# The first two row tiles of a split matrix product run side by side for five column tiles of the second weights instead of four

## The reference

```python
def _L0_cond_ref(x, weight, bias, lora_a_weights, lora_b_weights, scaling_factors, adapter_id):
    base = einsum('bsi,oi->bso', x, weight) + bias
    low = einsum('bsi,bri->bsr', x, lora_a_weights[adapter_id])
    delta = einsum('bsr,bor->bso', low, lora_b_weights[adapter_id])
    return base + scaling_factors[adapter_id][:, None, None] * delta

def _L0_ffn_ref(x, W_base, b_base, W_router, lora_A, lora_B):
    # softmax over 8 router logits, the two largest renormalised to w
    h = einsum('td,erd->ter', xf, lora_A)
    lora_out = einsum('ter,eor,te->to', h, lora_B, w) * 2.0
    return x @ W_base.T + b_base + lora_out

x = x + _L0_ffn_ref(_L0_cond_ref(x, ...), ...)
x = x + _L1_ffn_ref(_L1_cond_ref(x, ...), ...)     # the same form, other weights
```

## Time and profile before

| | us |
|---|---|
| median of 3 runs | 687.23 |
| lowest and highest run | 686.88 and 687.95 |
| time of the profiled execution | 687.59 |
| span of the profiled execution, first to last instruction | 685.8 |
| TensorE matmul busy | 680.0 |
| VectorE busy | 421.5 |
| POOL busy | 261.3 |
| ScalarE busy | 233.5 |

### The profile page before, as it was taken

One profiled execution on the slowest core, in us unless ns is written; L12 is line 12 of the kernel. 1 busy time (PEld: TensorE's weight loads), 2 busy tenths in 40 slices (PEclk: granted clock), 3 DMA queues, 4 the chain that ended last, 5 costly groups with the idle time before them and its releaser, 6 DMA issues.

```text
span 685.8 us, 9221 instructions
## 1 busy us (share of the span) xinstructions
PE 680.0 (99%) x3309; PEld 600.7 (88%) x3309; DVE 421.5 (61%) x705; ACT 233.5 (34%) x429; POOL 261.3 (38%) x217
## 2 busy tenths in 40 slices
PE   8999999999999999999999999999999999999997
PEld 7999999888888888888899999998888888888886
DVE  5664668768855473862663753886698437738423
ACT  6444245644131034220514344266252302422200
POOL 2373023027593150395133432030647625105920
PEclk9999999999999999999999999999999999999999
DMA  8355756992868934547742755689836886535633
GB/s 298 109 159 180 261 198 209 390 380 108 263 186 321 343 117 130 157 141 258 281 170 72 231 169 183 246 275 375 332 122 216 291 333 195 175 117 171 192 113 122
DMA packets 74131, 147.24 MB, mean 215 GB/s; under 512 B 6948, under 2 KB 38308, under 8 KB 73958
## 3 DMA queue, kind: packets, MB, share of 16 engines
q1 hardware_dynamic: 70678, 138.20, 59.0%
q10 hardware_dynamic: 1872, 6.36, 3.0%
q0 software_dynamic: 1536, 2.10, 1.1%
HBM read 98.42 MB, written 47.33 MB: 213 GB/s over the span
## 4 chain that ended last, share of the span: by engine, by line
PE 97%; DMA 1%; SPq 1%; ACT 0%; DVE 0%; issue 0%
PE ps L599 45%; PE ps L481 15%; PE ps L482 15%; PE ps L483 15%; PE ps L558 4%; PE ps L615 2%; DMA e_raw<-in_ext 1%; PE ps L608 1%; SPq L281 0%; PE ps L498 0%; PE ps L581 0%; ACT e_hl L710 0%; SPq L258 0%; DVE w_hl L972 0%; DVE w L1177 0%; ACT w_hl L719 0%
## 5 line engine op out<-in xcount | busy, mean ns | idle before, releaser
L599 PE MATMUL ps<-x_hl,a_hl 128*128 128x512 f32 x1344 | 317.7, 394 | 0.0
L599 PEld LDWEIGHTS ps<-x_hl,a_hl 128*128 128x128 f32 x1344 | 251.1, 188 | 53.6 <-issue 0.3
L481 PE MATMUL ps<-e_hl,w_hl 128*128 128x384 f32 (+1 forms) x432 | 145.8, 338 | 0.6 <-DVE e_hl L972 0.5
L482 PE MATMUL ps<-e_hl,w_hl 128*128 128x384 f32 (+1 forms) x432 | 145.8, 338 | 0.0
L483 PE MATMUL ps<-e_hl,w_hl 128*128 128x384 f32 (+1 forms) x432 | 145.6, 337 | 0.0
L481 PEld LDWEIGHTS ps<-e_hl,w_hl 128*128 128x128 f32 x432 | 81.5, 189 | 1.8 <-issue 1.0
L482 PEld LDWEIGHTS ps<-e_hl,w_hl 128*128 128x128 f32 x432 | 81.4, 188 | 0.0
L483 PEld LDWEIGHTS ps<-e_hl,w_hl 128*128 128x128 f32 x432 | 81.4, 188 | 0.0
L972 DVE TENSOR_TENSOR x_hl<-x_raw,x_hl 128x512 fp32r<-128x512 f32 x64 | 60.8, 1004 | 8.9 <-ACT x_hl L806 8.9
L1353 POOL TENSOR_TENSOR w<-x_raw 128x512 f32<-128x512 f32 x16 | 23.8, 1515 | 104.6 <-DMA x_raw<-in_xT 34.0
L972 DVE TENSOR_TENSOR w_hl<-w_raw,w_hl 128x1024 fp32r<-128x1024 f32 (+2 forms) x24 | 20.6, 869 | 57.2 <-ACT w_hl L697 50.3
(11 more groups left out here) (115 smaller groups left out, 900.1 us busy)
## 6 DMA issues: line engine op xcount, KB each, us to landing
a_hl<-form_scratch SPq DMA_DIRECT2D x112, 512.0 KB, 5.2
form_scratch<-f_hl SPq DMA_DIRECT2D x56, 512.0 KB, 7.4
e_raw<-in_ext SPq DMA_DIRECT2D x12, 580.0 KB, 8.6
w_raw<-in_w ACTq DMA_DIRECT2D x12, 512.0 KB, 3.3
x_raw<-in_xT SPq DMA_DIRECT2D x6, 1024.0 KB, 8.0
x_raw<-x_scratch SPq DMA_DIRECT2D x6, 1024.0 KB, 7.0
x_scratch<-x_raw SPq DMA_DIRECT2D x16, 256.0 KB, 3.1
out_T<-x_raw SPq DMA_DIRECT2D x16, 256.0 KB, 3.3
```

Of the source, the lines that this page charges most:

```text
L481: nc.tensor.matmul(dst, w_hi, m_hi, start=start, stop=False, skip_group_check=again)
L482: nc.tensor.matmul(dst, w_hi, m_lo, start=False, stop=False, skip_group_check=again)
L599: last = nc.tensor.matmul(ps[:, bank, :], a_hl[:, n % NM, k, w, :], x_hl[:, slot, k, x, :], start=start and i == 0, stop=i == 3 * KH - 1, ...
```

## The change

The bound between the mixed part and the two rests goes from 4 to 5, in the one loop that serves both layers:

```diff
-                for r, i in [(r, i) for i in range(4) for r in range(2)] + [(r, i) for r in range(2) for i in range(4, KT)]:
+                for r, i in [(r, i) for i in range(5) for r in range(2)] + [(r, i) for r in range(2) for i in range(5, KT)]:
```

## The result

The changed kernel takes 690.25 us (median of 6 runs, 689.83 to 690.47) against 687.59 us for the kernel before, run beside it (median of 6, 686.88 to 687.95). The ratio is 1.0038, with a 95% interval from 1.0028 to 1.0048: slower, by 2.66 us by the medians. The forecast was 689.8, with a range from 688.6 to 691.0, and 2.53 us of loss. Of the 0.45 us between forecast and median, 0.36 are the kernel before itself, whose median is 687.59 over six runs and was 687.23 over three. The profiled execution took 690.12 us with a span of 688.4; forecast were 690.1 and 688.4.

What follows compares the result with a forecast made beforehand. TensorE bounds the kernel, with a matmul under way for 680.0 of 685.8 us. With 0 gained and 1.29 + 1.24 us lost in the two layers, 687.23 + 2.53 = 689.8 us, range 688.6 to 691.0.

Steps and rivals of the forecast that it cites:

- the steps 05 to 07: Second-weights steps in both layers, made 1.58 us later: they don't wait today, so the gain is 0.
- Chain and cover: Reload of r = 2's first weights takes 6.06 and 6.01 us; TensorE's work meanwhile falls from 6.50 to 4.92.
- The tail: Extra after a wait ending on VectorE: 0.05 us to start, 0.10 at the second matmul, 0.15 a layer.
- The sum: Waits at r = 2: 1.29 us in layer 0 plus 1.24 in layer 1, 2.53 us lost, 0 gained.
- What is pushed further: Layer 0 after the delayed cast: copies and r = 3's weights about 0.75 us later, absorbed by 2.6 us room.
- The load did not land later: Rival: the reload of first weights lands 3.3 us later in one layer, time 693.1; chance 0.03.
- The not-slower case: Rival: layer 0's tile 5, 6 or 7 is late in ordinary executions, today's order stalls; 688.2; chance 0.05.
- The clock rival: Rival: the new pause drops TensorE's clock to 1.2 GHz, 2.7 us a layer, 695.1 in all; chance 0.03.

Runs made afterwards that it cites:

- the early load: Changed kernel's order (five tiles mixed), but row tile 2's first weights loaded early into a buffer of their own: 687.49 us, ratio 1.0002.

## Why the prediction was right

- **No gain from the steps 05 to 07.** They have no wait before and none after, and with three tiles mixed, where they come even earlier, the time doesn't change measurably. This held.
- **Chain and cover.** 6.06 and 6.01 us of chain against 4.92 of cover was the core of the sum. After, the chain is 6.13 (27.99 to 34.12) in layer 0 and 6.03 (366.39 to 372.42) in layer 1, the cover 4.92. The 0.07 us more in layer 0 are the load and its hand-over, 3.44 instead of 3.37.
- **The tail.** 0.05 us from VectorE's end to TensorE's start and 0.10 at the second matmul, read off one earlier wait, came back at each wait of r = 2: the second start is 0.27 to 0.29 us behind the first in all the kernels with a pause here and a fast clock.
- **The sum.** 1.29 + 1.24 forecast, 1.37 + 1.27 in the profile, 2.66 by the medians: 0.13 us too little, inside the narrower range of 689.0 to 690.9 that the prediction gives too. That the span came out at the very 688.4 that was forecast is partly luck, since the pauses are 0.11 us longer than forecast and layer 1 begins 1.02 us later in place of 1.3.
- **What is pushed further.** That r = 1's copies would run into the cast, and that r = 3's weights would come later without being missed, held. The path between the two was wrong. The first copy is 0.54 us late, but the third one had been waiting for TensorE anyway and absorbs this: it ends at 34.00 after and 34.14 before, so no delay reaches GpSimd's sums by way of the copies. Yet r = 3's cast starts at 42.24, 0.98 us later than its 41.26 in the kernel before, where 0.75 was forecast. That the two numbers lie near each other is luck: the 0.98 us come from VectorE and GpSimd (last section). The low part is ready at 44.55, r = 3 begins at 46.88, and of the forecast room of 2.6 us 2.3 is left.
- **The rivals.** The load did not land later (3.4 us median for its line, 3.3 before). The not-slower case, a late tile of the second weights, didn't appear. The clock rival was wrong for this change: behind pauses of 1.44 and 1.35 us between starts all matmuls stand 0.175 us apart. But it was no idle thought. One step further, with six tiles, it costs some 1.55 us in each layer, a third of the profiled execution's loss. The 2.7 us a layer by which it was priced, from the beginning of the program, are too much for that, and nearly what layer 1 pays with eight tiles (2.65). The Trainium skill (TensorE: Matmul & The Clock Gate, section HAM oscillation) tells of waits for DMAs that bring the slow clock back. The kernels with six and eight tiles agree (granted clock 0.50 behind pauses of 2.96 to 4.63 us), and the changed kernel shows that shorter pauses don't.

The kernel before stays the fastest here, with three tiles and with the early load beside it within the measurement. The waits left at its start, 13.43 to 17.18, are for data that are still arriving, and no order of the steps tried here brings step 03 ahead of 16.95.

## What to carry to other kernels

A loop order that keeps one consumer from waiting also sets when a buffer falls free; before mixing work more deeply, find what hangs on the end of the first item (here a reload of 6 us) and compare it with the work that is left behind it. Room and chain could be read off a timeline to 0.1 us here, up to 0.4 us of scatter in the load's landing aside, and the loss beyond the room is one for one, until the pause is long enough to bring the slow clock, from where it costs more. If the deeper mix is wanted, give the reload its own buffer: that took the chain from 6.1 to 3.5 us here.

## What the runs showed of the hardware

**Pauses and the clock.** Pauses in dense matmul work, measured between starts, with the clock behind them: 1.65 us (five tiles, layer 0 alone) and 1.97 (eight tiles, early load) leave it at 2.4 GHz; 2.96 and 3.32 (six tiles), 4.51 and 4.63 (eight tiles) drop it to 1.2 GHz. In three of these four the drop comes 0.6 to 0.9 us after the first matmul behind the pause, in one (4.51) within the pause. Between 1.97 and 2.96 lies one measurement, the 2.28 us ahead of step 03 with two tiles (14.92 to 17.20): in the profiled execution it leaves the clock at 2.4 GHz. A pause of a given length doesn't seem to have the same outcome each time. With six tiles the two executions of 694.5 us have a mean granted clock of 0.998, and the two of 696.1 and 696.6 have 0.995. With two tiles the two executions of 690.7 us have 0.998, the three of 688.9 to 689.2 have 1.000. As an estimate, 0.002 off the mean over 690 us are 2.8 us at half the clock, about one slow stretch, and 0.005 are two; the 1.5 to 2.1 us between the times fit that. Only one execution of each kernel has a trace, so where the slow stretches of the others lie isn't shown.

**VectorE and GpSimd hold each other up.** This explains the 0.98 us of r = 3's cast. GpSimd's first sum starts no later after the change than before it. What moved is VectorE's pair of sums of line 1033: it follows the low part of r = 2's weights, so it begins at 34.03 in place of 32.55, and takes 3.80 us in place of 2.88. Timeline of GpSimd in the kernel before, which answers to the one behind it:

```profile
34.22 2.36 POOL L1335 TENSOR_TENSOR f_sum<-p_raw 128x512 f32<-128x512 f32 x1 [1.31 <-ACT p_raw L755]
36.73 1.29 POOL L1338 TENSOR_TENSOR f_sum<-f_sum,p_raw 128x512 f32<-128x512 f32 x1
```

and in the kernel after:

```profile
34.08 2.52 POOL L1335 TENSOR_TENSOR f_sum<-p_raw 128x512 f32<-128x512 f32 x1 [1.35 <-ACT p_raw L755]
36.74 2.22 POOL L1338 TENSOR_TENSOR f_sum<-f_sum,p_raw 128x512 f32<-128x512 f32 x1
39.11 1.31 POOL L1341 TENSOR_TENSOR f_sum<-p_raw,f_sum 128x512 f32<-128x512 f32 x1
```

Before, VectorE's second sum (34.00 to 35.43) meets GpSimd's first one, and GpSimd's second one runs alone in 1.29 us. After, both of VectorE's sums meet GpSimd, and GpSimd's second one takes 2.22 us. These 0.93 us are what ScalarE's later casts, and r = 3's behind them, are late by. In the kernel with the early load VectorE's pair begins at 31.38 and is nearly over when GpSimd starts at 34.02, and GpSimd's two sums take 1.39 and 1.29 us. On VectorE the low part of 128 columns, 0.29 us alone, takes 1.38 beside GpSimd and ends 0.17 us behind GpSimd's second sum, at 39.13 (in the kernel before it takes 1.39 beside GpSimd's first one):

```profile
37.75 1.38 DVE L972 TENSOR_TENSOR px_hl<-p_raw,px_hl 128x128 fp32r<-128x128 f32 x1
```

The Trainium skill (SBUF — State Buffer, section SBUF: two separate sides) says that the two engines share one pair of ports, held by an instruction to its end, and that a VectorE operation with two inputs in SBUF contends for it with a GpSimd operation that reads SBUF. The rows agree: each waits for about one instruction of the other. It cost nothing here, since r = 3 had 2.3 us of room left, but the later low part changed who meets whom, and that added 0.93 us that no sum of the delays on ScalarE would give. No run moves one of the two engines alone, so the hold-up is read from these overlaps.
